# A two-layer graph attention kernel: x in 4 KB pieces, an earlier reference for layer 0's shift, gathers without a wait, and identity transposes in TensorE's waits

## The reference

```
h = relu(layernorm(x));  x = x + L0(h, W0, a0, adj)
h = relu(layernorm(x));  x = x + L1(h, adj, W1, a1)
L0: h = input @ W; e = leaky_relu((h @ a_src)[:, None] + (h @ a_dst)[None, :], 0.2)
    att = softmax(where(adj > 0 & valid, e, -1e9), axis=1), kept where att >= 1e-4
    attention = att * L[:, None]          # L: number of valid neighbours
    return elu(h + attention @ h)
L1: Wh = h @ W; the same e; attention = softmax(where(adj > 0, e, -9e15), axis=1)
    return attention @ Wh
```

## Time and profile before

| | us |
|---|---|
| median of 3 runs | 1978.59 (1973.93 to 1979.74) |
| profiled execution, its own time | 1969.02 |
| its span, first to last instruction | 1967.1 |
| around the span | 1.9 |
| first product of layer 0 (end of the opening) | 82.13 |
| TensorE busy in the span | 1906.6 (97%) |
| VectorE busy | 1740.1 (88%) |
| ScalarE busy | 1471.5 (75%) |
| GpSimd busy | 1242.6 (63%) |

### The profile page before, as it was taken

One profiled execution on the slowest core, in us unless ns is written; L12 is line 12 of the kernel. 1 busy time (PEld: TensorE's weight loads), 2 busy tenths in 40 slices (PEclk: granted clock), 3 DMA queues, 4 the chain that ended last, 5 costly groups with the idle time before them and its releaser, 6 DMA issues.

```text
span 1967.1 us, 39089 instructions
## 1 busy us (share of the span) xinstructions
PE 1906.6 (97%) x16858; PEld 1898.0 (96%) x16858; DVE 1740.1 (88%) x2023; ACT 1471.5 (75%) x1745; POOL 1242.6 (63%) x1010
## 2 busy tenths in 40 slices
PE   4789999999999999999999999999999999999998
PEld 3689999999999999999999999999999999999997
DVE  7888898998989899898969898998989899898985
ACT  4988897888889888898771877777788777778710
POOL 3675776767767575775640777767677676768600
PEclk9799999999999999999999999999999999999999
DMA  8999898899989788897990798888989788888900
GB/s 252 349 344 342 291 320 268 299 328 344 319 287 334 275 304 285 309 328 268 370 361 12 262 365 290 299 306 292 338 285 332 274 300 308 293 329 295 329 19 13
DMA packets 181381, 566.46 MB, mean 288 GB/s; under 512 B 18768, under 2 KB 49872, under 8 KB 179664
## 3 DMA queue, kind: packets, MB, share of 16 engines
q0 software_dynamic: 142848, 520.16, 74.9%
q1 hardware_dynamic: 33424, 41.36, 6.3%
q10 hardware_dynamic: 4928, 2.36, 0.5%
HBM read 548.01 MB, written 15.79 MB: 287 GB/s over the span
## 4 chain that ended last, share of the span: by engine, by line
PE 86%; DMA 5%; DVE 4%; ACT 2%; POOL 1%; issue 1%; SPq 0%; DVEq 0%; POOLq 0%
PE psum L766 84%; DMA arena<-in_adj_dram,piece_rows 4%; ACT arena L360 2%; PE psum L724 1%; DVE arena L1063 1%; POOL arena L350 1%; DVE arena L864 1%; DVE arena L378 1%; DMA arena<-x_mid 1%; PE psum L713 0%; DVE st L839 0%; DMA arena<-in_x_dram 0%; POOL piece_rows L396 0%; PE psum L691 0%; DVE h_all L885 0%
## 5 line engine op out<-in xcount | busy, mean ns | idle before, releaser
L766 PE MATMUL psum<-h_all,arena 128*128 128x129 f32 x16384 | 1841.6, 275 | 10.1 <-DVE arena L1063 10.0
L766 PEld LDWEIGHTS psum<-h_all,arena 128*128 128x128 f32 x16384 | 1836.4, 192 | 13.0 <-DVE arena L1063 10.3
L350 POOL DMA_INDIRECT arena<-in_adj_dram,piece_rows x992 | 1233.2, 1243 | 623.7 <-ACT arena L360 434.0
L360 ACT ACTIVATE arena<-arena,half_step 128x1024 uint8<-128x1024 int32 x992 | 1370.5, 1440 | 287.2 <-DMA arena<-in_adj_dram,piece_rows 156.5
L1063 DVE SCALAR_TENSOR_TENSOR arena<-arena,sd_col 128x1024 f32<-128x1024 f32 x512 | 641.2, 1277 | 103.1 <-PE psum L766 98.4
L1063 DVE SCALAR_TENSOR_TENSOR arena<-arena,rho_col 128x1024 f32<-128x1024 f32 x448 | 563.5, 1278 | 69.3 <-PE psum L766 66.3
L378 DVE STREAM_TRANSPOSE arena<-arena 128x1024 f32<-128x1024 f32 x248 | 306.0, 1235 | 8.7 <-ACT arena L360 8.4
L360 ACT ACTIVATION_READ_ACCUMULATOR arena<-arena,half_step 128x1 f32 x512 | 92.5, 181 | 0.0
L1063 DVE SCALAR_TENSOR_TENSOR arena<-psum,rho_col,arena 128x1024 f32<-128x1024 f32 x64 | 79.1, 1267 | 6.8 <-PE psum L766 6.6
L724 PE MATMUL psum<-W_ext,arena 128*128 128x131 f32 x256 | 38.5, 313 | 13.5 <-DVE h_all L885 10.0
L724 PEld LDWEIGHTS psum<-W_ext,arena 128*128 128x128 f32 x256 | 36.3, 224 | 14.9 <-issue 10.6
(11 more groups left out here) (126 smaller groups left out, 195.1 us busy)
## 6 DMA issues: line engine op xcount, KB each, us to landing
arena<-in_adj_dram,piece_rows POOLq DMA_INDIRECT x992, 5.9
arena<-in_x_dram SPq DMA_DIRECT2D x48, 128.0 KB, 5.8
x_mid<-arena SPq DMA_DIRECT2D x8, 512.0 KB, 6.9
edgesT<-arena SPq DMA_DIRECT2D x4, 1024.0 KB, 9.1
arena<-edgesT SPq DMA_DIRECT2D x4, 1024.0 KB, 16.8
arena<-x_mid SPq DMA_DIRECT2D x8, 512.0 KB, 6.6
out_dram<-arena SPq DMA_DIRECT2D x28, 128.0 KB, 11.3
h_mid<-arena SPq DMA_DIRECT2D x6, 512.0 KB, 3.0
```

The lines of the kernel that those rows point to most:

```text
L350: pool.indirect_dma_start(adj_in[n % NA], None, adj_pieces, bass.IndirectOffsetOnAxis(ap=piece_rows[:, column:column + 1], axis=0))\
L360: nc.scalar.activation(pack_bytes[h][:, k, a], adj_in[n % NA], ACT.Sign, bias=half_step[:, 0:1], accum_out=into).then_inc(masked, 1)
L766: last = nc.tensor.matmul(acc_tile(g, k), wTs[m % RING][:, k * P:(k + 1) * P], h_all[:, j, 0:FZ], start=(j == 0 and k % 2 == 0), stop=(j = ...
```

## The change

Seven things are changed together.

1. x comes in four pairs of parts. A DMA carries 32 partitions with two runs of 4 KB, so that node 8m + u of a quarter lies in partition m. The transposed parts therefore hold their columns in another order, and the copies out of PSUM put it right: four copies of 128 x 8 x 32 elements, with a stride, in place of one of 128 x 1024.
2. GpSimd's gathers wait for x no more.
3. The weights of layer 1 are loaded behind all of x.
4. Layer 0 is shifted by a reference too: the largest d of part 0. VectorE finds it right behind `keep_h(0)`, in three steps on end. The products of part 1 wait for it on TensorE (`ref_ready`).
5. r of group 0 is formed early: ScalarE's `first_r(0, G)` stands ahead of mask 14 (FIRST_R), VectorE's `limit_r` behind `keep_h(2)`, its transposition on TensorE ahead of the products of part 3, which also wait for `rows_ready`; the row goes through DRAM and back (`load_r(4, ...)`), and the diagonal and its products are gone.
6. The true extremes of layer 0 are found while group 0 is summed (tiles 9, 15 and 21), with one more check, and the exponentials that need them follow on ScalarE ahead of mask 64.
7. TensorE transposes the identity eight times ahead of its wait for each normalised part from 2 on, and 32 times behind the last products.

```diff
-            pool.wait_ge(x_loaded[XP // 2 - 1], 16 * BK)
             for n in range(len(PASSES) * PIECES):
                 load_piece(pool, n)
-                if n == 2:
-                    pool.wait_ge(x_loaded[XP - 1], 16 * BK)
...
+        def load_x(eng, pair, which):
+            two = x_all[:, 2 * pair * TP:(2 * pair + 2) * TP, :].rearrange("p (i u) f -> p i (u f)", i=2)
+            for b in (2 * which, 2 * which + 1):
+                eng.dma_start(two[b * BP:(b + 1) * BP], eight_rows(pair, b)).then_inc(x_loaded[pair], 16)
...
             load_weights(0, W0, a0)
-            for i in range(XP):
-                load_x(sp, i, 0)
-                if i == 3:
-                    load_weights(1, W1, a1)
-            store_r(0, 0, T)
+            for pair in range(XP // 2):
+                load_x(sp, pair, 0)
+            load_weights(1, W1, a1)
+            sp.wait_ge(z_turned[0], 1)
+            store_r(0, 0, G)
+            load_r(4, slice(0, GW))
+            store_r(1, G, T)
             load_r(0, slice(GW, 3 * GW))
...
-                nc.scalar.activation(zTs[i % 2], zT_ps(0, i), ACT.Relu).then_inc(zT_ready[0], 1)
+                for b in range(BK):
+                    last = nc.scalar.activation(ordered_rows(zTs[i % 2], b), turned_rows(i, b), ACT.Relu)
+                last.then_inc(zT_ready[0], 1)
...
+            def first_r(t0, t1):
+                nc.scalar.activation(r_col[:, t0:t1], sd_col[:, t0:t1, 0], ACT.Exp, scale=ALPHA - 1.0,
+                                     bias=exp_bias[:, 1:2]).then_inc(r_ready, 1)
...
             def exps():
-                act.wait_ge(lin_ready, 1)
-                nc.scalar.activation(r_col[:], lin[:], ACT.Exp, scale=ALPHA - 1.0).then_inc(r_ready, 1)
+                act.wait_ge(first_sd_kept, 2)
...
+                if i == FIRST_R:
+                    act.wait_ge(ref_ready, 1)
+                    first_r(0, G)
...
-                pe.wait_ge(z_ready[layer], i + 1)
                 if layer == 0 and i >= 2:
                     pe.wait_ge(zT_ready[0], i - 1)
+                    for t in range(TP):
+                        nc.tensor.transpose(zT_ps(0, i)[:, t * P:(t + 1) * P], ident[:], ident[:])
+                pe.wait_ge(z_ready[layer], i + 1)
...
+                if i == 1:
+                    turn_extremes(0, first_spread_ps)
+                    spread_extremes(0, first_spread_ps)
+                    pe.wait_ge(ref_ready, 1)
+                if i == 3:
+                    turn_r(0, r_col, first_rT_ps, 0, G)
+                    pe.wait_ge(rows_ready, 1)
                 products(0, i)
...
+            pe.wait_ge(zT_ready[0], XP)
+            for t in range(4 * TP):
+                nc.tensor.transpose(zT_ps(0, t // TP)[:, t % TP * P:(t % TP + 1) * P], ident[:], ident[:])
...
             keep_h(0)
+            for step in range(3):
+                find_reference(0, step)
+            normalise(0, 4, x_part(4), x_part(4))
             keep_h(1)
-            normalise(0, 4, x_part(4), x_part(4))
+            normalise(0, 5, x_part(5), x_part(5))
             keep_h(2)
-            normalise(0, 5, x_part(5), x_part(5))
-            keep_h(3)
+            limit_r(r_col, r_ready, 1, 0, G)
             dve.wait_ge(zT_ready[0], 4)
             keep_zT(4)
+            keep_rows(0, first_rT_ps, G)
             normalise(0, 6, x_part(6), x_part(6))
+            keep_h(3)
...
-            extreme_values()
-            diagonals()
+            dve.wait_ge(h_kept[0], 2 * XP)
+            keep_sd(G, T).then_inc(first_sd_kept, 2)
             dve.wait_ge(exps_ready, 1)
             fold(0)
             turn_edges(dve, 0, 1, 0)
-            dve.wait_ge(r_spread, 1)
+            dve.wait_ge(r_loaded[4], 16)
```

More of the change, by code:

```diff
@@ L208, in kernel_program @@
         set_up = sem(p + "vector_set_up")
-        x_loaded = [sem(p + f"x_loaded{i}") for i in range(XP)]
+        x_loaded = [sem(p + f"x_loaded{i}") for i in range(XP // 2)]
         w_loaded = [sem(p + f"w_loaded{i}") for i in range(2)]
@@ L238, in kernel_program @@
         r_stored = sem(p + "r_stored")
-        r_loaded = [sem(p + f"r_loaded{i}") for i in range(4)]
+        r_loaded = [sem(p + f"r_loaded{i}") for i in range(5)]
         ref_ready = sem(p + "ref_ready")
@@ L637, in scalar_fast @@
             zT_at = {3: 0, 4: 1, 7: 2, 8: 3}
-            for i in range(XP):
-                load_x(act, i, 1)
+            for pair in range(XP // 2):
+                load_x(act, pair, 1)
             act.wait_ge(set_up, 1)
@@ L879, in keep_zT @@
                     dve.wait_ge(h_done[0], 2 * (i - 1))
-                nc.vector.tensor_scalar(zTs[i % 2], zT_ps(0, i), 0.0, None, ALU.max).then_inc(zT_ready[0], 1)
+                for b in range(BK):
+                    last = nc.vector.tensor_scalar(ordered_rows(zTs[i % 2], b), turned_rows(i, b), 0.0, None, ALU.max)
+                last.then_inc(zT_ready[0], 1)
             def keep_h(i):
```

211 lines of the change are left out of this document (113 added, 98 removed).

## The result

| | median of the runs | profiled execution | its span | mean clock |
|---|---|---|---|---|
| before | 1976.3 us (1967.5 to 1979.7, 4 runs) | 1969.0 | 1967.1 | 0.991 |
| after | 1998.7 us (1992.8 to 2002.4, 4 runs) | 2002.4 | 2000.6 | 0.987 |

The ratio is 1.0108 (95% interval 1.0082 to 1.0134): the change makes the kernel slower by 1.1%, some 22 us. The forecast was 1987.4, slower too, but by 8.8 only; 1998.7 lies above its range. The sign was right and the size was not. The two terms that were mis-sized the most had been put near zero.

What follows compares the result with a forecast made beforehand. TensorE bounds the kernel behind the opening, where the chain runs through ScalarE's masks; 1.1 + 8.5 + 2.8 - 3.6 = +8.8 us on the median 1978.6 gives 1987.4 us, own range 1983 to 1991, overall 1979 to 1996.

Steps and rivals of the forecast that it cites:

- It comes along ScalarE's masks: Chain through ScalarE's masks releases TensorE at 135.67; claim: the end stays as far behind the 64th mask as before.
- masks 31 to 64: ScalarE's masks from the 31st to the 64th, fed by gathers: no change, 0 us, bounds -8.6 and +3.
- x and the weights, up to K: Opening up to K, VectorE's start of keep_h(0): weights land later, x no longer waited for; +1.1 us, bounds -2.6 and +5.
- Gathers without a wait: ScalarE's first mask starts about 17 instead of 24.32; the 7 us lead ends in waiting for part 3; 0 us.
- The reference: VectorE's copy, reduction and scalars after keep_h(0) take 2.6 us; then TensorE's products of part 1 take 3.7 us.
- Part 3 and the wait for r: VectorE waits 7 to 8 us at limit_r for ScalarE; first transposed copy +8.5 us, bounds +3 and +11.
- To the last copy of h: From first transposed copy to last copy of h: smaller copies, row and identities; net +2.8 us, bounds +1 and +5.
- To the 31st mask: From last copy of h to 31st mask: copy, hand-over, three exponentials, 1.2 us instead of 4.8; -3.6 us.
- Rival B: Full clock and early x: keep_h(0) 2 us earlier or unmoved; +2.2 to +4 us, 1981.8 in the middle; chance 0.2.
- C: ScalarE's lead survives part 3's copy and TensorE's wait at tile 26 goes; -9.3 us, 1969.3; chance 0.07.
- Rival D: Identities do not hold clock; weights late; keep_h(0) and later stretch +5 each; +14.9 us, 1993.5; chance 0.18.
- The signs: Expected in the changed profile: first statistics near 10, VectorE idle about 7 us at L980, tile 26 wait ending near 144.

Runs made afterwards that it cites:

- experiment 6: Kernel before with x in 4 KB pieces and four copies for each part, nothing else: 1980.4 us, 1.0018.
- gated_gathers: Changed kernel with GpSimd's two waits for x brought back ahead of the first and fourth gathers: 1994.4 us, 1.0092.
- experiment 7: Two versions of the changed kernel: FIRST_R = 8 instead of 14, 1997.3 us; ScalarE's copy of part 3 behind its 14th mask, not its 8th, 1991.1 us.
- experiment 10: Kernel before with row numbers made ahead of the first gather and next layer's part 6 copied behind 25 masks: 1962.9 us; the part 6 edit alone: 1969.1 us.
- experiment 9: Also spelled rows_first: changed kernel with all of GpSimd's row numbers made ahead of the first gather, 1987.8 us, 1.0052.
- experiment 8: Changed kernel without TensorE's turns of the identity: 1999.2 us, 1.0121.
- experiment 1: Changed kernel with group 0's r copied from SBUF into PSUM and read there by VectorE's tiles: 1987.2 us, 1.0055.

## Why the prediction was wrong in size

- **"It comes along ScalarE's masks ... releases TensorE at 135.67"**, the rule by which I added up: right. Tile 26's release moved by 20.8 us and the median by 22.5, and the wait was still there (12.94 us). But the chain was read from its last rows only; a little earlier it ran through iotas and gathers, and there the term of masks 31 to 64 was to be looked for.
- **"x and the weights, up to K: +1.1", bounds -2.6 and +5: the first failed step.** +7.3. The weights at 7.78 and the price of 4 KB pieces were near (first statistics forecast 10.2, came 11.37; K +2.3 in experiment 6). But the sum said "From then on VectorE no longer waits for x", having set the bytes of x against all 16 engines; gathers were counted beside small packets only. The runs show what they cost the whole of x: +4.9 in after, +7.9 in before.
- **"Gathers without a wait. ... I cost it at nothing."** I looked only at what ScalarE's lead would bring, which was indeed nothing: from K to the 31st mask it is 45.3 us with the lead and without it (gated_gathers). The cost was on the side of the transfers beside it.
- **"The reference", 2.6 us**: 2.7 (45.16 to 47.86); products of part 1 3.86 for 3.7. Right.
- **"Part 3 and the wait for r: +8.5"**: the transposed copy came 8.0 later against K, with the idle 7.13 at L980 as forecast. Every row was there, and the reason I drew from it was half wrong: the term was booked as VectorE's wait, but ScalarE, equally full, was on the path beside it (experiment 7). An experiment built on my text would have removed FIRST_R's wait and got 1.5 us.
- **"To the last copy of h: +2.8"**: +1.0, inside +1 to +5. **"To the 31st mask: -3.6"**: -3.6 (4.8 to 1.2). Together with the above the stretch K to 31st mask was forecast +7.7 and came +5.4. These 2.3 us made up for a part of the two failed terms, by luck.
- **"Masks 31 to 64. 34 of them, as before. ... 0, bounds -8.6 and +3": the second failed step.** +8.1. I followed counts, bytes and iotas, but not the one operand that moved: VectorE's tiles read r from SBUF, not PSUM. That costs VectorE itself next to nothing (1277 ns a tile for 1267), so its rows gave no hint; GpSimd pays. And "the eight iotas behind gather 48 stay" was no reason for nothing: they held up the masks in before already (3.9 us, experiment 10), and beside slower gathers they cost more (7.3, experiment 9). With r in PSUM the term is -1.1 (55.6 for 56.7), with the iotas gone +0.8. The trace of before had the comparison in it: group 0's gathers with r in PSUM took 0.95 us, and those of later groups, with r in SBUF, some 1.3.
- **Rival B** (early x) and **C** (ScalarE's lead survives) did not come. **Rival D** was nearest in time (1993.5) with K at +5 and its stretch at +5, but that is a coincidence: the identities did hold the clock higher from 70 to 86 and it changed nothing in the time (experiment 8), and 8.1 of the measured delay lie in masks 31 to 64, which D put at nothing.
- **The signs.** First statistics at 11.37, VectorE's 7.13 us at L980 and the wait at tile 26 came as forecast. One sign failed that K does not explain: ScalarE was to stand idle ahead of `D_col` for some 6 us, and it did for 0.76. It had no slack there, which is what experiment 7 then found.

What stays open: that K of rows_first came 3.2 us earlier, where 0 to 2 were expected, was not taken apart; what decides whether a gather is blocked (of the 17 profiles 16 have one of 7.9 to 9.3 us between 993 and 1031, and that of before has none); and why r's place costs after 9.2 us and the kernel before at most 2.8.

## What to carry to other kernels

When an operand moves between PSUM and SBUF, ask who else uses the port, not only how long the reader takes: here a tile went from 1267 to 1277 ns and the neighbour's gather from 0.95 to 2.2 us in the stretch that counts. Prefetching into an opening that waits for its own inputs is paid for by those inputs; put instead the work without transfers (row numbers) into that wait. And when two engines wait side by side, the one with the larger or more visible wait need not be on the path: look for the engine that has next to no gap between its wait and the end of the stretch.

## What the runs showed of the hardware

- A gather instruction of GpSimd made no headway during seven VectorE instructions in a row with two SBUF inputs and ended 0.82 us after them (9.32 us in all). Others beside the same kind of instruction took their usual 0.94 us, so it does not happen to each.
- The Trainium skill's "SBUF — State Buffer" (Who interferes with whom) names this contention between instructions; that it suffices to read one of the two inputs from PSUM is shown by experiment 1: 942 ns a gather in the mean, beside a VectorE that is busy 9.1 to 10 of each 10 us from 100 to 140.
- 512-byte pieces suffer more from gathers beside them than 4 KB ones: 7.9 against 4.9 us of delay for the same 4.2 MB, from one profile each.
